# One core, six changes: order of the first tables, first transposes, sixteen weight buffers, eight widths, and TensorE in loops of sixteen experts

## The reference

```
x = x + L0_ffn(einsum('bct,bcd->bdt', x, W0[subject]) + bias0[subject])   # 8 subjects
  L0_ffn: alpha = softmax(relu(x W1 + b1) W2 + b2); sum_k alpha_k U_k (V_k x)   # 8 kernels of rank 64
x = x + L1_ffn(x W[id] + b[id])                                            # 16 matrices of 256 x 256
  L1_ffn: softmax over 64 experts, the 6 best, weights renormalised;
          each expert takes at most CAP = 384 rows;
          expert: silu(x wg) * (x wu) wd, 256 -> 176 -> 256; sum back by token
          plus one shared expert 256 -> 352 -> 256 for all tokens
```

## Time and profile before

| | |
|---|---|
| median of 3 runs | 540.35 us (537.68 to 542.27) |
| the profiled execution | 540.61 us, span 538.9 us |
| mean granted TensorE clock | 0.973 |
| TensorE busy | 490.7 us |
| VectorE, ScalarE, POOL busy | 297.8, 187.6, 300.3 us |
| four groups | 0 to about 151 us |
| shared expert | about 151 to 210 us |
| experts | 213 to 513 us |
| reading back, adding, storing | to 538.9 us |

### The profile page before, as it was taken

One profiled execution on the slowest core, in us unless ns is written; L12 is line 12 of the kernel. 1 busy time (PEld: TensorE's weight loads), 2 busy tenths in 40 slices (PEclk: granted clock), 3 DMA queues, 4 the chain that ended last, 5 costly groups with the idle time before them and its releaser, 6 DMA issues.

```text
span 538.9 us, 10609 instructions
## 1 busy us (share of the span) xinstructions
PE 490.7 (91%) x2505; PEld 361.4 (67%) x2505; DVE 297.8 (55%) x825; ACT 187.6 (35%) x398; POOL 300.3 (56%) x249
## 2 busy tenths in 40 slices
PE   1979999999999998899999999999899999999940
PEld 1525536464456554778889888888888787989730
DVE  7733856748488213535456555654666455546435
ACT  0121223212130111434455545554555454546300
POOL 4001047777677770247767666566657556768540
PEclk9979999999999999999999999999999999999985
DMA  5865969879734953689899999998999999855389
GB/s 169 272 187 189 368 205 310 277 238 308 248 146 133 357 195 95 180 192 211 201 239 240 232 246 218 262 234 197 254 252 244 236 221 210 198 106 85 37 182 321
DMA packets 88184, 117.17 MB, mean 217 GB/s; under 512 B 14464, under 2 KB 74288, under 8 KB 88112
## 3 DMA queue, kind: packets, MB, share of 16 engines
q1 hardware_dynamic: 55456, 57.05, 34.7%
q0 software_dynamic: 21840, 30.18, 27.2%
q10 hardware_dynamic: 10816, 28.97, 17.2%
HBM read 78.88 MB, written 39.16 MB: 219 GB/s over the span
## 4 chain that ended last, share of the span: by engine, by line
PE 85%; DVE 6%; issue 3%; DMA 3%; ACT 1%; POOLq 0%; SPq 0%; POOL 0%; DVEq 0%; ACTq 0%
PE bank L1133 28%; PE bank L1158 10%; PE bank L1157 10%; PE bank L1064 8%; PE bank L985 6%; PE bank L1101 6%; PE bank L919 4%; PE bank L1077 3%; PE bank L1002 3%; PE bank L931 2%; PE bank L1017 1%; DVE sil L665 1%; PE bank L948 1%; DMA cw<-acc 1%; DMA acc<-OH,sids 1%
## 5 line engine op out<-in xcount | busy, mean ns | idle before, releaser
L513 POOL DMA_INDIRECT acc<-sil,sids x64 | 97.6, 1525 | 68.4 <-ACT sil L612 34.6
L496 POOL DMA_INDIRECT slot_rows<-ctok,sli x96 | 97.4, 1014 | 56.0 <-issue 28.1
L513 POOL DMA_INDIRECT acc<-OH,sids x63 | 96.1, 1526 | 55.3 <-issue 35.6
L882 DVE TENSOR_TENSOR hh<-sg,bank 48x384 f32<-48x384 f32 x64 | 35.6, 556 | 59.7 <-ACT sg L599 48.6
L612 ACT ACTIVATE sil<-bank,wcol 128x256 f32<-128x256 f32 x64 | 29.7, 474 | 52.4 <-PE bank L1158 51.2
L612 ACT ACTIVATE OH<-bank,wcol 128x256 f32<-128x256 f32 x64 | 29.8, 474 | 49.6 <-PE bank L1158 47.8
L597 ACT ACTIVATE sg<-bank 128x384 f32<-128x384 f32 x64 | 31.5, 491 | 36.8 <-PE bank L1133 35.4
L1064 PE MATMUL bank<-cTs,sgus 128*128 128x512 f32 (+1 forms) x96 | 42.2, 593 | 0.5 <-ACT base L544 0.5
L1101 PE MATMUL bank<-ident,cw 128*128 128x128 f32 x276 | 40.7, 273 | 2.0 <-DVE xgT L856 2.0
L1101 PEld LDWEIGHTS bank<-ident,cw 128*128 128x128 f32 x276 | 34.1, 141 | 9.0 <-issue 2.8
L884 DVE TENSOR_TENSOR hh<-sg,bank 128x384 f32<-128x384 f32 x64 | 35.5, 555 | 2.6
(11 more groups left out here) (227 smaller groups left out, 925.8 us busy)
## 6 DMA issues: line engine op xcount, KB each, us to landing
cw<-in_cW SPq DMA_DIRECT2D x64, 256.0 KB, 4.0
cw<-slot_rows SPq DMA_DIRECT2D x94, 136.0 KB
wb<-in_wblk ACTq DMA_DIRECT2D x10, 496.0 KB, 4.1
slot_rows<-blank SPq DMA_DIRECT2D x72, 68.0 KB, 3.6
acc<-zrow POOLq DMA_DIRECT2D x2, 2048.0 KB
cw<-acc SPq DMA_DIRECT2D x8, 512.0 KB, 6.1
bd<-in_wblk ACTq DMA_DIRECT2D x8, 496.0 KB
z<-in_wblk ACTq DMA_DIRECT2D x8, 496.0 KB, 4.2
```

Source lines behind the costliest of these rows:

```text
L496: pool.indirect_dma_start(slots_d, bass.IndirectOffsetOnAxis(sli[:, g % 2, k, t:t + 1], 0), ctok[:, g % 2, t, :], None, bounds_check=SLOTS ...
L513: pool.indirect_dma_start(acc[u % 2], bass.IndirectOffsetOnAxis(sids[0:rows, u % SR, j:j + 1], 0), yo[u % UE][0:rows, j, :], None, bounds_ ...
L882: v.tensor_tensor(hh[0:FT, u % 2, 1, :], sg[0:FT, 1, :], bank[4][CU:CU + FT, 0:CAP], ALU.mult).then_inc(s_hh, 1)
```

## The change

Six edits.

1. VectorE fills `bd` for group 0 before the bias parts. `mix` multiplies x first and adds the bias last, and waits for the bias only there. `cb3`, `ohb` and the bias table of groups 1 to 3 move into group 0: behind `als`, between the second and third product with spread, and behind the fourth.
2. The transposes of expert 0 stand between the second and third chunk of the last group of the shared expert. Two tiles of the last `shared_down` move into step 0, one stands before the last `down`, one behind it.
3. 16 weight buffers instead of 12; the four new ones lie in `cw` behind the experts' rows.
4. Eight widths instead of four.
5. TensorE's steps: step 0, then a loop of 16 steps run three times, then 15 steps written out.
6. PSUM banks, waits and memsets that follow from these.

```diff
-NW = 12
+NW = 16
-WIDTHS = [160, 224, 288, CAP]
+WIDTHS = [128, 160, 192, 224, 256, 288, 320, CAP]
+PR = 16
...
+        past_rows = cw_flat[:, UE * TJ * RW:]
+        wb += [past_rows[:, i * WROW:(i + 1) * WROW] for i in range(4)]
...
+        wt_later += [past_rows[:, 4 * WROW + i * D:4 * WROW + (i + 1) * D] for i in range(3)] + [wt_more[:, 2, :]]
...
-        SDB = [(7, 6), (0, 1)]
+        SDB = [(7, 6), (7, 0)]
...
+        def first_then_rounds(eng, step, forget):
+
+            step(0, 0, first=True)
+            with eng.Fori(0, E // PR - 1) as i:
+                forget()
+                for u in range(1, PR + 1):
+                    step(i * PR + u, u)
+            forget()
+            for e in range(E - PR + 1, E):
+                step(e, e)
...
+            dve.wait_ge(s_wall, 16 * (BT + 1))
+            mixing(0, TG)
             link(v.tensor_copy(fs3[0:NS0, :], fs_s[:, :]))
...
             biases(0, BG)
-            mixing(0, TG)
             mixed(0)
             mixing(TG, TT)
-            biases(BG, B)
-
-            v.tensor_scalar(ohb[:, :, :], f_b1[:, :].unsqueeze(2).to_broadcast([K3, B, S]), pm[:, 0:1], None, ALU.is_equal)
...
                 if g:
                     slots_begun()
+                else:
+                    cond_bias()
                 for c in range(KC):
                     if g and c == 2:
                         slots_summed(g - 1)
+                    elif c == 2:
+                        v.tensor_scalar(ohb[:, :, :], f_b1[:, :].unsqueeze(2).to_broadcast([K3, B, S]), pm[:, 0:1], None, ALU.is_equal).then_inc(s_cb3, 1)
...
+                if g == 0:
+                    biases(BG, B)
...
                 for c in range(DC):
-                    mm(bank[c][:, :], onesb[0:K3, :], bias0[:, g * BG:(g + 1) * BG, :].rearrange("p b s -> p (b s)"),
-                       start=True, stop=False)
                     for t in range(TG):
-                        last = mm(bank[c][:, t * P:(t + 1) * P], x_g[:, t, c * P:(c + 1) * P], bd[:, g * TG + t, :],
-                                  start=False, stop=t == TG - 1)
-                    last.then_inc(s_mix, 1)
+                        mm(bank[c][:, t * P:(t + 1) * P], x_g[:, t, c * P:(c + 1) * P], bd[:, g * TG + t, :], start=t == 0, stop=False)
+                    if g == 0:
+                        pe.wait_ge(s_bias0, 1)
+                    mm(bank[c][:, :], onesb[0:K3, :], bias0[:, g * BG:(g + 1) * BG, :].rearrange("p b s -> p (b s)"),
+                       start=False, stop=True).then_inc(s_mix, 1)
...
-                pe.wait_ge(s_wb[b], 32 * (e // NW + 1))
+                pe.wait_ge(s_wb[b], 32 // NW * (e - u % NW) + 32)
...
+                if first:
+                    shared_down(G - 1, [0, 1])
...
+                if u == 0:
+                    pe.wait_ge(s_sb, 2 * (G - 1) + 1)
...
+            for g in range(1, G):
+                shared_chunk(g, 1)
+                if g == G - 1:
+                    pe.wait_ge(s_flags, 2)
+                    pe.wait_ge(s_hs, len(SCH) * g + 1)
+                    pe.sem_inc(s_tick, 1)
+                    tokens(0, 0)
+                shared_chunk(g, 2)
+                if g < G - 1:
+                    shared_chunk(g + 1, 0)
+                    shared_down(g, range(TG))
             tokens(1, 1)
             pe.wait_ge(s_hs, len(SCH) * G)
             pe.wait_ge(s_sb, 2 * (G - 1))
-            all_steps(step)
-            shared_down(G - 1, [0])
+            first_then_rounds(pe, step, forget)
+            shared_down(G - 1, [2])
             down(E - 1, E - 1)
-            shared_down(G - 1, range(1, TG))
+            shared_down(G - 1, [3])
```

## The result

The changed kernel takes 572.18 us (median of 4 runs, 570.25 to 576.23), the kernel before 539.01 (4 runs, 536.70 to 542.27). The ratio is 1.0603, with a 95% interval of 1.0549 to 1.0656. I had forecast 533 with a range of 527 to 541, and had given a chance of 0.11 to the mechanism that decided it.

A forecast was written before the change was run, and what follows sets the result against it. TensorE's work and gaps were taken as the bound. From 540.6 us, start -7.3, hand-over +0.6 and +1.3, widths -6, scatters +1.5 and loops +2.5 gave -7.4, so 533.2, or 533 against the median; range 527 to 541.

The forecast's parts named there:

- the mechanism that decided it: Expert steps: code fetch becomes the limit because eight variants lengthen the code; 25 us over 62 steps, 558 us, chance 0.11.
- Code fetch: Expert steps: a 16 KB piece of code needed every 4.3 us instead of every 7; 0.4 us standing per step assumed.
- Loops, +2.5, bounds 0 to 8: TensorE's expert loop: back-edges cost 2.5 us in the sum, with one longer step each at experts 17 and 33.
- Widths, -6: Expert steps: 896 fewer columns at 9.9 ns give 8.9 us, less 3 us for a third branch; -6 us taken.
- the rival that I had at 0.11: Expert steps: each stands 0.4 us for its piece of code, 25 us over 62 steps, 558 us; chance 0.11.
- Start, -7.3 with bounds -4.1 and -7.5: Before the experts: earlier mixing 0.6 us, no gap before alpha transposes 4.1, no low clock behind it 3.2; -7.3 us.
- Hand-over, +0.6 and +1.3: Shared expert to experts: last chunk ends later, +0.6 us; step 0 takes two shared_down tiles, 6.0 us between gates, +1.3.
- Scatters, +1.5: GpSimd in the expert steps: scatters begin to push back through four output buffers at 4.3 us a step; +1.5 us.
- Sixteen buffers, 0: Expert stage: weights are never waited for, so four more buffers hide nothing; 0 us.
- three low places in the page's row of the clock: Profile page of the kernel before: TensorE's clock is low at three places, one early, one in the middle, one at the end.
- The signs named beforehand: Signs of fetch and loops: about 77 code pieces instead of 47, TensorE idle at gates, longer steps at experts 17 and 33.

The follow-up runs named there:

- run 1: The changed kernel with TensorE's loops of 16 experts written out again, eight widths kept; ratio 1.0227 to the kernel before.
- run 4: The changed kernel with 32 experts per loop body instead of 16, so the loop runs once without a back-edge; ratio 1.0217 to the kernel before.
- run 3: The kernel before with eight widths instead of four and nothing else, no loop; ratio 1.0269.
- run 8: The kernel before with the conditional layer's tables built late and five widths (160, 192, 240, 288, 384), written out; 532.56 us, ratio 0.9849.
- run 5: The kernel before with four more widths that no expert ever uses (32, 48, 64, 80); 556.54 against 540.70 us, ratio 1.0306.
- run 9: The kernel before with the change's hand-over alone (tokens(0) between chunks, half of the last shared_down in step 0); ratio 1.0026.
- run 2: The changed kernel with the four old widths, loops kept; ratio 1.0125 to the kernel before.
- runs 9 to 12: On one chip: the kernel before with hand-over alone, with late tables and six widths, and twice unchanged; ratios 1.0026 and 0.9950, then 651.08 and 649.54 us.
- runs 1 to 4: On one chip: changed kernel with loops written out, or four widths; kernel before with eight widths; changed kernel with loop run once; ratios 1.0227, 1.0125, 1.0269, 1.0217.
- run 11: The kernel before, unchanged, profiled once more on one of the slower chips; 651.08 us.

## Why the prediction was wrong, step by step

**Code fetch** is where it failed, in two terms: the sum let each back-edge be nearly covered, and it held nothing for steps that wait for their code.

*Loops, +2.5, bounds 0 to 8.* Measured 23.1 from gate to gate against run 1, 17.2 against run 4 and 20.4 by medians (33.2 over the kernel before, run 1 12.8), each outside my bounds. I had priced a back-edge by a load's landing time, 4.1 us, and then let the sequencer's lead cover most of it. The branch itself does take 4.1 to 4.8 us. But little covers it, for the gate of the next step stands behind it and the matmuls queued ahead last 1.0 and 1.7 us; the steps beside it lose more, 9 us per back-edge: a second piece of code is missing two matmuls into the gate, and gate_up then runs at the lower clock, which no term of mine held. With four widths, where the second piece isn't missed and more matmuls are queued, it is 5.6. At all four back-edges in the traces the branch (4.13 to 4.76 us) ends 1.3 to 1.5 us behind the landing of a 16 KB piece, whose packet took 0.9 to 1.0 us. The sequencer's lead, which I had put at up to 2 us, is 1.1 us in the median and 3.2 at most in the trace of before, from the end of a branch between the row tiles (line 1166) to the next weight load of `down`.

*Widths, -6.* Measured +9.4 (run 1) to +15 (run 3). The steps with their code at hand are as I had them: 4.76 us at width 256 and 4.12 at 192 behind two tiles, as the starts below show, and 3.77 at 128 (461.78 to 465.55):

```profile
486.21 2.75 PE L1150 MATMUL bank<-xgT,VTs 128*128 128x256 f32 x12
490.97 2.12 PE L1150 MATMUL bank<-xgT,UTs 128*128 128x192 f32 x12
495.09 1.82 PE L1150 MATMUL bank<-x_g,x1T 128*128 128x160 f32 x12
```

What took the gain is the rival that I had at 0.11, with 25 us: stalls at about every third step, of 1 to 2.4 us in the change, not 0.4 at each. Its price of 25 us over 62 steps was too high without the loops: run 1 shows 15.4, the 9.4 lost and the 6 that the widths should have given. My evidence against it was that a piece moves in 1.1 us and that no gap of before falls to one. Both were true and said nothing of the changed kernel: what counts is the 1.4 us more between a piece's landing and the branch's end, and how soon the sequencer, leaping over seven of eight variants, wants the next piece. Apart from the back-edges it never waited over 0.6 us at one piece every 7 us or more, did so twice at one every 6.5 (run 8), and does so 15 to 25 times at one every 5.7 to 4.6; run 5 shows that the length of the code alone does it.

**Start, -7.3 with bounds -4.1 and -7.5.** Measured -3.7, just outside. The gap and the low clock at 32 us (0.50 for 6.8 us before) went as foreseen. Two things in front of them were missed. The bias chain became so late that TensorE stood 1.7 us for it: casts that took 0.17 us each before took 0.68 and 1.32 beside GpSimd's memsets. Both end 0.03 us after a memset does (11.66 and 11.63, 13.02 and 12.99), and the five traces with this order have the same durations; that the memsets hold them up is read from this, not tested. And half of the first layer ran at half its speed, 5.55 us in all. I had summed against one execution in which TensorE sped up at about 15 us, and taken that for the program's.

**Hand-over, +0.6 and +1.3.** Measured 1.5 in the change (3.74 won ahead of it, 2.27 left at gate 1), 1.45 in run 9. The sum is right to 0.5 by luck, for both halves are wrong. Ahead of gate 0 2.0 us are lost, not 0.6; 0.86 of it is the wait for expert 0's rows, which I had at 0.2. Gate 0 to gate 1 is 4.46 us, 0.5 less than before, not 6.0; 1.0 of the difference is the gate, which ran at the high clock (1.59 us, not 2.6). Nothing was gained at the end: the scatters outlast TensorE. There GpSimd's last scatter and TensorE's last matmuls stand so:

```profile
543.64 1.46 PE L1101 MATMUL bank<-sds,hs 128*128 128x256 f32 x6
...
548.32 1.43 POOL L530 DMA_INDIRECT acc<-OH,sids  x1 [0.30 <-issue]
```

**Scatters, +1.5.** Measured 0. GpSimd idles more, waiting for ScalarE; before, ScalarE waited for it twice (1.2 us in the expert steps, 1.8 behind them), now never. But the steps never reached the pace of 4.3 us for which the term stood, so it is untested and not refuted.

**Sixteen buffers, 0.** Right: in run 2, which has them, the 58 other steps are those of before.

**A reading.** The prediction sees three low places in the page's row of the clock. The row shows two; the middle one, a mean of 0.62 from 212.0 to 216.5 us, is too short for it. No term hangs on this.

The signs named beforehand were the right ones: about 77 pieces (78 came), long steps at the loop's rounds, TensorE idle at gates with VectorE done. The chances weren't.

## What to carry to other kernels

Price the code, not only the work: count the instructions that a step leaps over, and ask how many microseconds lie between two 16 KB boundaries. Here one boundary in 7 us was free, and with one in 4.6 to 4.8 us the 62 steps took 9 to 15 us longer, loops aside; six and eight widths lost more than they gave. A back-edge on the engine that sets the pace costs 5.6 to 9 us here. What the loops of eight on SP and GpSimd cost, which both kernels have, wasn't measured. When one execution is the base of a sum, look in a second one for what moves between them.

## What the runs showed of the hardware that I had not expected

- A branch that waits for code ends 1.3 to 1.6 us after the piece has landed, in all 128 long branches of the eight traces that have any. The packet itself takes 0.9 to 2.0 us there, up to 2.5 in all traces. Where the branch seems to ask for the piece itself, at the four back-edges, 1.75 to 2.4 us more pass before the packet starts, 4.1 to 4.8 us in all (run 2: branch 401.09, packet 402.84 to 403.73, end 405.22). From these times I estimate that a piece has to be asked for some 4 us ahead here, not the 1.1 us that it moves.
- TensorE can be at half speed without the row of its clock telling. In the window

```profile
17.80:21.50 3.70, 3.67 (x5) 1.63 (x6) 3.49 (x7) 0.00 (x0) 0.00 (x0) 1.00 0.86 273
```

  the granted clock reads 1.00, and five matmuls fill 3.67 us (the first four start 0.85 us apart, the last three of the layer 0.43); before, eight of the same form took as long. The profile's first record of the clock in this trace stands only at 21.62 us, so the row has nothing to tell of the time before. The duration has to be read beside the clock. And the moment at which the first matmuls get faster isn't fixed: in traces with the late tables the first conditional matmul comes at 38.1 or 40.6, in those of the kernel before at 44.8, 44.9 or 46.8, the code up to there being the same.
- The chip of runs 9 to 12 needs what the chip of the first trace needs for the expert stage, to 0.3%, but the stages ahead of it take about 110 us longer there, and on that of runs 1 to 4. In run 11 TensorE is busy for 230 us up to the end of the shared expert, not 193, and idle for 79 us behind 20 us, not 4; its granted clock stands at 0.50 for 119 us of that stretch, not 7, in turns of some 31 us between 92 and 242 us. VectorE and ScalarE wait for `ctok` up to 24 us at a time, which the trace ascribes to no engine. What comes first there stays open.
